# Reordering a head's sixth step and moving the value tiles' high halves to ScalarE in a cross-attention and mixture-of-experts kernel

## The reference, cut to what matters

```python
x = layer_norm(x, ...); lat = layer_norm(latents, ...)
q = lat @ Wq
kv = concatenate([x, lat], axis=1) @ Wkv
k, v = split(kv, 2, axis=-1)                # 16 heads x 64
attn = softmax(einsum('bhid,bhjd->bhij', q, k) * scale)
out = einsum('bhij,bhjd->bhid', attn, v) ... @ Wout
x = x + out;  x = x + expert_of(token)(layer_norm(x))
```

## Time and profile before

| | us |
|---|---|
| median of 3 runs | 2175.25 (2172.24 to 2176.8) |
| the profiled execution | 2173.39 |
| its span, first to last instruction | 2171.7 |
| mean granted TensorE clock | 0.975 |
| head to head in the attention, by the profile | about 25.3 to 26.2 |

### The profile page before, as it was taken

One profiled execution on the slowest core, in us unless ns is written; L12 is line 12 of the kernel. 1 busy time (PEld: TensorE's weight loads), 2 busy tenths in 40 slices (PEclk: granted clock), 3 DMA queues, 4 the chain that ended last, 5 costly groups with the idle time before them and its releaser, 6 DMA issues. The chain is left out here.

```text
span 2171.7 us, 63039 instructions
## 1 busy us (share of the span) xinstructions
PE 2010.2 (93%) x25468; PEld 1367.3 (63%) x25468; DVE 1615.2 (74%) x3115; ACT 1472.5 (68%) x1835; POOL 1421.1 (65%) x803
## 2 busy tenths in 40 slices
PE   2799999999999999999999999999999998589997
PEld 2266666667666666667666666676666665567675
DVE  7677777777778888777788887777888874745554
ACT  4277777776677777766777777767777777156664
POOL 3078888884688877865877788748878877023232
PEclk9699999999999999999999999999999999789999
DMA  5122222222222222222222222222222221271110
GB/s 167 37 53 53 53 54 63 53 55 59 68 58 54 53 53 53 59 54 70 53 58 63 54 53 53 49 71 54 62 54 54 53 62 28 94 302 37 44 44 27
DMA packets 127505, 137.92 MB, mean 64 GB/s; under 512 B 45538, under 2 KB 92310, under 8 KB 126070
## 3 DMA queue, kind: packets, MB, share of 16 engines
q1 hardware_dynamic: 123477, 124.49, 22.3%
q0 software_dynamic: 3744, 9.39, 1.4%
HBM read 53.06 MB, written 26.15 MB: 36 GB/s over the span
## 5 line engine op out<-in xcount | busy, mean ns | idle before, releaser
L708 POOL TENSOR_TENSOR probs_split<-probs,probs_split 128x1024 f16<-128x1024 f32 x576 | 1222.8, 2136 | 363.2 <-ACT probs_split L793 362.1
L786 ACT ACTIVATE probs<-score 128x1024 f32<-128x1024 f32 (+1 forms) x640 | 655.9, 1025 | 397.4 <-PE score L1076 386.8
L931 DVE TENSOR_REDUCE max_parts<-aux 128x1 f32<-128x512 f32 x1024 | 683.1, 688 | 101.7 <-PE aux L1076 93.5
L793 ACT ACTIVATE probs_split<-score 128x1024 f16<-128x1024 f32 (+1 forms) x640 | 652.0, 1019 | 0.0
L1172 PE MATMUL acc<-values,probs_split 128*128 128x65 f16 x5120 | 554.7, 193 | 8.2 <-POOL probs_split L708 8.0
L1176 PE MATMUL acc<-values,probs_split 128*128 128x64 f16 x4608 | 519.8, 194 | 0.0
L1177 PE MATMUL acc<-values,probs_split 128*128 128x65 f16 x4608 | 517.6, 192 | 0.0
L1172 PEld LDWEIGHTS acc<-values,probs_split 128*128 128x128 f16 x5120 | 464.0, 97 | 64.5 <-POOL probs_split L708 11.7
L1076 PE MATMUL score<-q_both,k_high 128*128 128x512 f16 (+1 forms) x1280 | 485.7, 379 | 10.6 <-DMA q_max<-max_row 7.8
L1076 PE MATMUL aux<-k_high,q_both 128*128 128x512 f16 (+1 forms) x1536 | 461.9, 335 | 33.0 <-DVE values L927 20.6
L1076 PE MATMUL score<-q_max,k_low 65*128 65x512 f16 (+1 forms) x1280 | 488.6, 382 | 0.0
(11 more groups left out here) (170 smaller groups left out, 2242.7 us busy)
## 6 DMA issues: line engine op xcount, KB each, us to landing
k_high<-raw SPq DMA_DIRECT2D x128, 147.2 KB, 2.5
q_both<-raw SPq DMA_DIRECT2D x128, 128.0 KB, 2.5
piece_in<-in_L_ffn_W SPq DMA_DIRECT2D x64, 256.0 KB, 3.1
halves<-piece_out SPq DMA_DIRECT2D x128, 128.0 KB, 2.4
k_low<-raw SPq DMA_DIRECT2D x64, 147.2 KB, 2.4
q_max<-raw SPq DMA_DIRECT2D x64, 128.0 KB, 2.5
w<-halves SPq DMA_DIRECT2D x16, 512.0 KB
w<-halves SPq DMA_DIRECT2D x8, 1024.0 KB
```

The source lines that it names most:

```text
L708: nc.gpsimd.tensor_tensor(out=low[0:r, :], in0=prob(h, j)[0:r, :], in1=high[0:r, :], op=ALU.subtract)\
L786: nc.scalar.activation(prob(h, j)[0:r, :], score[j % 2][0:r, :], ACT.Exp, scale=SCALE)\
L793: nc.scalar.activation(halves(h, j)[0][0:r, :], score[j % 2][0:r, :], ACT.Exp, scale=SCALE)\
L931: nc.vector.tensor_reduce(max_parts[g % 2][:, t, c:c + 1], bank[:, :], AX.X, ALU.max)\
```

## The change

Three edits. In step 5 (the sixth) of every head the places change from (none, v, turn, first) to (none, turn, first, v). The cast to the high half of every "v" chunk, those of BEFORE too, moves from VectorE to ScalarE. There it stands in step j behind `exponent` when the chunk has place 0 or 1 (step 7), and behind `high_half` when it has place 2 or 3 (step 5). VectorE keeps the low half, and now waits for ScalarE's semaphore.

```diff
-    ("", "v", "turn", "first"),
+    ("", "turn", "first", "v"),
...
+            def value_high(chunk):
+
+                _, pair, g = chunk
+                act.wait_ge(aux_full, NUMBER[chunk] + 1)
+                if g == 0:
+                    at_least(act, av_done, 2 * JT * 2 * (pair - 1))
+                nc.scalar.activation(value_half(pair, g, 0), value_bank(bank_of(chunk), g), ACT.Copy).then_inc(values_high, 1)
+
             def head(h):
                 for j in range(JT):
                     of, jj = tile_ahead(h, j)
                     if of < HEADS:
                         exponent(of, jj)
+                    early, late = [[c for c in BESIDE[h][j][at:at + 2] if c and c[0] == "v"] for at in (0, 2)]
+                    for chunk in early:
+                        value_high(chunk)
+                    if of < HEADS:
                         high_half(of, jj)
+
+                    for chunk in late:
+                        value_high(chunk)
...
+            for chunk in BEFORE:
+                if chunk[0] == "v":
+                    value_high(chunk)
             for j in range(AHEAD):
...
                 elif kind == "v":
                     dve.wait_ge(aux_full, number + 1)
-                    if chunk[2] == 0:
-                        at_least(dve, av_done, 2 * JT * 2 * (g - 1))
-                    nc.vector.tensor_copy(value_half(g, chunk[2], 0), value_bank(bank, chunk[2])).then_inc(values_high, 1)
                     dve.wait_ge(values_high, len(VALUE_TILES) * g + chunk[2] + 1)
```

## The result

| | before | changed |
|---|---|---|
| median, us | 2174.84 (2172.24 to 2176.8, 4 runs) | 2140.55 (2138.39 to 2142.98, 4 runs) |
| profiled execution, us | 2173.39 | 2138.39 |
| its span, us | 2171.7 | 2136.6 |

The ratio is 0.9843 with a 95% interval of 0.9826 to 0.9860: 34 us less, or 1.6%, where the forecast was 36.7 (2138; the prediction's 2136.7 + 1.9 is 2138.6). The five later runs of the changed kernel had a median of 2140.88.

A forecast was written before the change was run, and what follows sets the result against it. TensorE, busy 93%, was taken as the bound, with only holes in its starts recoverable. Terms 17.9 + 10.8 + 5.0 + 4.5 - 1.5 gave 36.7 us off 2173.39, 2136.7, plus 1.9 for the median: 2138, range 2124 to 2156.

The forecast's parts named there:

- TensorE's holes are the loss: Attention heads: time is saved only at gaps in TensorE's starts; ordinary heads lose 0.54 + 0.40 or 0.28 + 0.29 us.
- the 0.05: Step 5, three-tile heads: loss charged per head, 31 in all, because the bank's hand-off had no margin.
- The copy's price: ScalarE's cast of a values chunk's high half: 0.50 us for 384 columns, 0.39 for 256.
- the line between two rows: ScalarE's copy time read on a straight line from 0.28 us (128 columns) to 0.93 us (896 columns).
- the 1.5 us set aside for it: Deduction in the sum for the nil margin of the bank's hand-off: 31 x 0.05 us.
- Step 7's room: Values bank in step 7: freed at 622.71, needed at 622.78, 0.07 us to spare; some 0.05 with two tiles.
- The slower rival: ScalarE's strided copy costs 1.0 us, the bank comes 0.55 later at 124 places: +58 us, 2196; chance 0.05.
- Gate heads: 24 heads with the gate's work: step 5's 0.62 hole becomes 0.59 awaiting the turn's copy, step 8's goes; 5.0 us.
- the 0.1 for "xt": Three-tile gate heads: VectorE takes the low half so late that "xt" waits some 0.1 us for a maximum.
- The maxima's DMA: Maxima copied earlier give their DMA 1.4 us more; its 7.8 us of waits nearly vanish, counted as 4.5.
- The 0.38 that stays: Two-tile heads, before step 8's first chunk: 0.38 us awaiting step 7's maximum behind tile 9's split, untouched by the change.
- SyncE issues the same instructions in the same order: Under the maxima: SyncE's queue is unchanged and nothing before `send_max` waits longer; no cost charged.

The follow-up runs named there:

- e1: Kernel before with only step 5's new order (turn, first, values), the casts left on VectorE: 2160.95 us, ratio 0.9935.
- e2: Changed kernel with step 5's old order, so only the casts moved to ScalarE: 2163.71 us, ratio 0.9948 to before.
- e6: Changed kernel with ScalarE's copy of each values chunk made twice, the first into a spare tile: 2151.02 us, ratio 0.9891 to before.
- e3: Changed kernel with a separate semaphore for the two small context-key copies, so maxima await only the first four arranging DMAs: 2131.99 us, ratio 0.9799 to before.
- e9: Changed kernel with VectorE's normalisation of rows in gate heads moved behind the turn's copy: 2132.39 us, ratio 0.9811 to before.
- e7: Changed kernel with VectorE's split of tile 9 moved behind step 7's first maximum: 2130.32 us, ratio 0.9791 to before.
- e4: Changed kernel with step 5's maximum moved to step 9, which then has three: 2145.19 us, ratio 0.9866 to before.

## Why the prediction was right

- **TensorE's holes are the loss.** Right. Of the two edits the order closes step 5 (e1) and the cast step 8 (e2), at 2161 and 2164, 2 us from their forecasts. In ordinary heads a pair (three tiles, two tiles) went from 25.37 + 25.34 to 24.70 + 24.48 us where no DMA was awaited: 1.53 less, forecast 1.51 less the 0.05. That the sum fits is partly luck: step 5 gave 0.57 and 0.32 instead of 0.54 and 0.28 and the other starts came some 0.08 closer together, while the hole in front of step 8 grew from 0.38 to 0.51.
- **The copy's price.** 0.49 and 0.38 us; the line between two rows gave 0.50 and 0.39. By the page "VectorE: DVE Perf Modes" of the Trainium skill (section on the TRN2 errata) an estimate is 0.46 and 0.36; what was measured lies nearer to the line. The hand-off had other parts than laid out (0.04 from the chunk's end to ScalarE, 0.10 on to VectorE, instead of 0.14 and 0.06) with nearly the same sum. The room came out at 0.04 instead of -0.01 (e6), so the 1.5 us set aside for it were not lost.
- **Step 7's room was misread.** The prediction weighed 0.07 us for the bank and let the slow copy cost at 124 places. The low half waits there for the maximum ahead of it on VectorE (477.42 against 477.91), so the copy has 0.4 to 0.5 us more. In step 5 of ordinary two-tile heads a later bank is hidden by the wait in front of step 8. Only the 31 places of step 5 in three-tile heads pay in full. The slower rival was overpriced about threefold: e6 with 0.39 more of ScalarE cost 10.5 us and not 25 to 36.
- **Gate heads** were undersized. From turn to turn they took 25.89 and 26.19 before; without the DMA's wait (e3) 25.92 and 25.39, 0.77 a pair and 9 us in all, where the sum had 0.42 a pair and 5.0. The hole for the turn's copy was 0.51 and not 0.59, so step 5 gave 0.14 with two tiles and not 0.03. With three tiles it gave 0.07 and step 8's hole of 0.21 closed, 0.28 and not 0.1; the 0.1 for "xt" did not appear. That the new hole awaits the turn's copy, late behind line 977, is shown by e9.
- **The maxima's DMA.** Its wait is nearly gone; what that gave by itself was not measured apart. 19 x 1.53 + 12 x 0.77 make 38.3 of the 42.5 us between before and e3, and the 4.2 left are about the 4.5 that the sum had for it.
- **The 0.38 that stays.** It stayed, in part of these heads with a length of 0.51, and e7 shows whose it was: the maximum's place behind the split. That the split itself gets longer beside GpSimd's work was not foreseen.
- **The step that failed:** "SyncE issues the same instructions in the same order", under the maxima, looked at one DMA only. The chunk that was moved up has a wait of its own, for the six arranging DMAs, and 1.3 to 1.9 us earlier it met them: 8 to 9 us (e3). The mechanism of the gain was right, but that the number came so close is luck. Two errors of the sum, this one and the undersized gate heads (4.2) with the unneeded 1.5, nearly cancelled: 36.7 forecast, 34 measured, about 43 without that wait.

## What to carry to other kernels

When a job is moved to an earlier place, list everything that this job itself waits for, its transfers above all, and not only who waits for its result. Where two banks alternate, count for each job which one is two places behind it, and price the order and the engine of the evacuation apart: here one edit without the other gave 13 and 11 us, both 34. A hole that opens behind the start of a chain that is awaited later costs nothing until it is longer than that wait.

## What the runs showed of the hardware

ScalarE started a copy of a finished bank 0.04 us after the matmuls' recorded end (472.75 to 472.79, and so in 52 of the 53 copies that waited for the chunk alone), while exponents start 0.14 after theirs (614.82 to 614.96); the code has a semaphore increment of ScalarE's own between the latter's wait and the exponent, and whether that is the cause was not tried. Six DMAs of one queue, issued 0.6 us apart, were all landed only about 3 us after the last one's issue had ended (573.10 to 576.08).

VectorE's split of tile 9 has one shape, 32x1024, in every head and takes 1.22 us where it overlaps GpSimd's subtraction of line 708 by 0.14 us or less. Where it starts earlier it ends 1.08 us after GpSimd does, whatever its start: 1.33 to 1.34 us with an overlap of 0.25 (9 heads of the changed kernel), 1.38 to 1.40 with 0.31 (10 heads of e9), 1.54 to 1.56 with 0.47 (19 heads of e4), 1.60 to 1.61 with 0.53 (12 heads of e4). Apart from this stand two splits near the end of the attention in each kernel and one of e4's, during which GpSimd begins its next instruction. GpSimd's own instructions keep their 2.1 to 2.2 us. So work that comes earlier on VectorE can get longer there. That GpSimd is the cause is read from these ends; no run moved its work to test it.
